# Heads: each step's products for the maxima stand behind the scores and the weighted sums

## The reference, cut to what matters

```python
def _L1_gnn_ref(x, adjacency, W_q, W_k, W_v, W_o, b_o):
    q = (x @ W_q).reshape(8, 2048, 4, 32).transpose(0, 2, 1, 3)
    k = (x @ W_k).reshape(8, 2048, 4, 32).transpose(0, 2, 1, 3)
    v = (x @ W_v).reshape(8, 2048, 4, 32).transpose(0, 2, 1, 3)
    scores = jnp.einsum('bhnd,bhmd->bhnm', q, k) / np.sqrt(32)
    scores = jnp.where(adjacency == 0, -jnp.inf, scores)
    attn = jax.nn.softmax(scores, axis=-1)
    out = jnp.einsum('bhnm,bhmd->bhnd', attn, v)
    return out.transpose(0, 2, 1, 3).reshape(8, 2048, 128) @ W_o + b_o

# layer 0: adjacency attention with scores that are sums of two node values
# layer 1:
h = jnp.maximum(_layernorm(x, axis=-1), 0.0)
x = x + _L1_gnn_ref(h, adj, ...)
# layers 2 and 3: mean over neighbours; adjacency attention again
```

## Time and profile before

| what | us |
|---|---|
| median of 3 runs (lowest, highest) | 3532.34 (3532.33, 3533.17) |
| the profiled execution | 3530.73 |
| its span, first to last instruction | 3528.9 |
| TensorE busy, products | 3409.4 (97%) |
| TensorE busy, weight loads | 1790.0 (51%) |
| VectorE busy | 3066.7 (87%) |
| GpSimd busy | 1830.4 (52%) |
| ScalarE busy | 1808.0 (51%) |
| the stage `heads`, first to last product | about 762 to 2643 |

### The profile page before, as it was taken

One profiled execution on the slowest core, in us unless ns is written; L12 is line 12 of the kernel. 1 busy time (PEld: TensorE's weight loads), 2 busy tenths in 40 slices (PEclk: granted clock), 3 DMA queues, 4 the chain that ended last, 5 costly groups with the idle time before them and its releaser, 6 DMA issues. The chain is left out here.

```text
span 3528.9 us, 58152 instructions
## 1 busy us (share of the span) xinstructions
PE 3409.4 (97%) x21140; PEld 1790.0 (51%) x21155; DVE 3066.7 (87%) x6862; ACT 1808.0 (51%) x4044; POOL 1830.4 (52%) x922
## 2 busy tenths in 40 slices
PE   6899998889999999999999999999998999899999
PEld 6799998431111111111111111111116999899999
DVE  8899997579999999999999999999977776677777
ACT  8633543766666666666666666666662554310010
POOL 7400101238888888888888888888870111000000
PEclk9999999999999999999999999999998999999999
DMA  8612121940011011101110111010003331312120
GB/s 301 220 69 91 55 91 54 291 161 10 25 30 30 8 27 30 30 6 29 30 30 5 30 30 30 6 30 30 6 7 108 120 120 73 121 67 91 55 91 25
DMA packets 78816, 234.62 MB, mean 66 GB/s; under 512 B 13504, under 2 KB 40768, under 8 KB 64448
## 3 DMA queue, kind: packets, MB, share of 16 engines
q1 hardware_dynamic: 77808, 230.56, 19.5%
q10 hardware_dynamic: 720, 0.33, 0.0%
HBM read 148.85 MB, written 81.99 MB: 65 GB/s over the span
## 5 line engine op out<-in xcount | busy, mean ns | idle before, releaser
L1828 POOL TENSOR_TENSOR a_w<-a_w,keep_mask_t 128x1024 f32<-128x1024 f32 x760 | 1608.0, 2141 | 306.1 <-ACT a_w L1813 306.1
L1813 ACT ACTIVATE a_w<-a_sc_ps 128x512 f32<-128x512 f32 x2048 | 1111.4, 595 | 705.1 <-PE a_sc_ps L1734 703.5
L1712 PE MATMUL a_o_ps<-a_w,a_v 128*33 128x512 f32 x4096 | 1079.1, 605 | 0.2
L1191 PE MATMUL g_acc<-g_hv,g_w 128*128 128x129 f32 x8192 | 923.2, 276 | 16.6 <-DVE g_w L1036 16.6
L1191 PEld LDWEIGHTS g_acc<-g_hv,g_w 128*128 128x128 f32 x8192 | 920.8, 193 | 17.9 <-ACT g_hv L1069 13.3
L1767 DVE CUSTOM_DVE_ANT_0 a_mx_ps<-a_mx_ps,a_mbias 128x512 f32<-128x512 f32 x1024 | 673.9, 718 | 39.5 <-PE a_mx_ps L1696 39.0
L1767 DVE CUSTOM_DVE_ANT_0 a_mx_ps<-a_mx_ps,em_mbias 128x512 f32<-128x512 f32 x968 | 636.5, 718 | 30.1 <-PE a_mx_ps L1696 29.8
L1734 PE MATMUL a_sc_ps<-a_qs,a_ks 97*128 97x512 f16 x2048 | 621.8, 385 | 0.5 <-ACT a_w L1813 0.2
L1780 DVE TENSOR_TENSOR a_w<-a_w,keep_mask_t 128x1024 f32<-128x1024 f32 x264 | 468.6, 1775 | 22.0 <-ACT a_w L1813 16.6
L1696 PEld LDWEIGHTS a_mx_ps<-a_ks,a_qs 32*128 32x128 f16 x1992 | 88.8, 91 | 784.9 <-DVE a_mx L1767 428.0
L1036 DVE SCALAR_TENSOR_TENSOR g_w<-f_row,keep_s,keep_mask_t 128x1024 f32<-128x1024 f32 x256 | 331.9, 1318 | 71.7 <-PE g_acc L1191 67.7
(11 more groups left out here) (313 smaller groups left out, 2383.2 us busy)
## 6 DMA issues: line engine op xcount, KB each, us to landing
p_adj_in<-in_adj SPq DMA_DIRECT2D x16, 1024.0 KB, 8.8
v<-p_v SPq DMA_DIRECT2D x32, 264.0 KB, 3.2
a_v<-v SPq DMA_DIRECT2D x16, 528.0 KB, 3.6
f_row<-u_rows SPq DMA_DIRECT2D x16, 512.0 KB, 5.9
g_x<-in_x SPq DMA_DIRECT2D x8, 1024.0 KB, 11.2
g_row<-u_rows SPq DMA_DIRECT2D x16, 512.0 KB, 8.1
x<-ho_o SPq DMA_DIRECT2D x16, 512.0 KB, 3.0
a_ks<-k_hi SPq DMA_DIRECT2D x64, 128.0 KB, 2.9
```

Of the source, the lines that this page charges most:

```text
L1191: mm = nc.tensor.matmul(tile(half, it), w[:, g % PB, it * P:(it + 1) * P], hv[:, k, jt, :], start=(jt == 0 and it % 3 == 0), stop=(jt == T ...
L1712: mm = nc.tensor.matmul(o_ps[2 * HD * a:2 * HD * a + HD + 1, c % 2, :], v[u][:, jt, a, :], w[:, g % PB, a, :], start=(jt == 0), stop=(jt = ...
L1813: nc.scalar.activation(w[:, g % PB, a], sc_ps[:, n % SB], ACT.Exp, scale=SCALE).then_inc(exp_done, 1)
L1828: nc.gpsimd.tensor_tensor(w[:, g % PB], w[:, g % PB], keep["mask_t"][:, jt, c * BANK:(c + 1) * BANK].unsqueeze(1).to_broadcast([P, 2, BANK ...
```

## The change

In the step loop of TensorE the first slot of a step was issued in front of its scores, and any further slot behind its weighing. Now all slots of a step are issued behind its weighing. The wait for the queries and keys of the next pair (`qk_loaded`) stays in front of everything, the wait for the placed shifts (`shift_placed`) stays in front of the scores. The code of the other engines is the same. The numbers of lines behind L1727 go down by one: the scores are L1733, the maximum on VectorE L1766, its mask L1779, the exponentials L1812, GpSimd's mask L1827.

```diff
@@ -1724,7 +1724,6 @@
                     if jt == 0 and tc == 0 and chunk < CHUNKS * B:
                         pe.wait_ge(qk_loaded[tu], LOADS * (i + on + 1))
                     mine_now = of_step(jt)
-                    slot(mine_now[0], chunk, tu, tc)
                     if jt == 0:
                         pe.wait_ge(shift_placed, 32 * (CHUNKS * i + g // T + 1))
                     for a in range(2):
@@ -1738,7 +1737,7 @@
                         weigh(g - LAG, i)
                     elif i > 0:
                         weigh(BODY + g - LAG, i - 1)
-                    for k in mine_now[1:]:
+                    for k in mine_now:
                         slot(k, chunk, tu, tc)
```

## The result

| | before | after |
|---|---|---|
| median of 5 runs, us | 3532.34 (3529.83 to 3533.57) | 3549.01 (3547.35 to 3551.49) |
| profiled execution, its span | 3530.73, 3528.9 | 3548.99, 3547.1 |
| the stage, start of its first to start of its last product | 1881.5 | 1897.1 |

The ratio is 1.0047, with an interval of 1.0036 to 1.0058: slower by 17 us. Of the 18.3 us between the profiled executions 15.6 lie in the stage, 0.6 ahead of it and 2.0 behind it.

The account below looks back on a forecast made before the run. TensorE's own stream was taken to bound the kernel. Only the steps around the turn cost, 63 x 0.21 = +13.3 us on 3530.73, giving 3544.0; 1.6 to the median made it 3545.6, say 3546, range 3537 to 3584.

Parts of the forecast that it names:

- (a): Ordinary steps on TensorE: the three gaps between products stay, so 14 of 16 steps cost what they did; cost 0.
- (b): Steps around the turn of the row maxima, on TensorE: 0.21 us more per chunk, 63 times, +13.3 us.
- T to M4: Gap from the turn of row maxima to step 4's maxima products: 0.20 or 0.21 us claimed, 63 times.
- (c, d): VectorE's mask asks at +1.49 us after step 2's scores, 0.16 before GpSimd, and takes 1.22; cost 0.
- rival 3: GpSimd takes the shared ports first, VectorE waits a whole instruction and TensorE waits: +330 us, 3862 us; chance 0.08.
- (e): Step 4's maxima products need step 3's maximum on VectorE taken first, for its buffer: slack 0.11 us, cost 0.
- rival 2: Step 3's maxima on VectorE are late at the turn: 63 x 0.2 to 0.7 more, 3558 to 3590; chance 0.14.
- (f): Shifts' DMA, placed some 1.4 us later, stays covered; the stage's start and end cost below 0.5 us.
- The sum: Whole kernel: profiled 3530.73 + 13.3 = 3544.0 us; as that execution lies 1.6 below the median, 3545.6, say 3546.
- Rival 1: The weight load of step 4's maxima products hides under the turn, gap 0.11: +7 us, 3539; chance 0.13.
- Rival 4: Faster: part of the 0.99 from weighing to maxima products waits for VectorE; -28, some 3518 us; chance 0.05.
- W to M: Gap on TensorE from the weighing to the maxima products, 0.98 or 0.99 us; claimed to hold no wait for VectorE.

Follow-up runs that it names:

- E2: Changed kernel with the small turn of the row maxima put between its step's scores and weighing; 3546.32 us, ratio 1.0038.
- E7: Kernel with maxima products in pairs and the turn between scores and weighing, GpSimd masking only one of two heads; 3491.07 us, ratio 0.9882.
- E6: Changed kernel, VectorE's masks also waiting for the second exponential of the next step, asking 0.03 ahead of GpSimd; 3555.37 us, ratio 1.0060.
- E5: Changed kernel, VectorE's masks also waiting for the first exponential two steps later, when GpSimd holds the ports; 3915.26 us, ratio 1.1082.
- E4: Changed kernel with a 128x256 memset on VectorE ahead of each of its masks; 3557.81 us, ratio 1.0071.
- E3: Kernel before, with GpSimd multiplying the mask onto only one of two heads; 3531.66 us, ratio 0.9996.
- E1: Changed kernel with the turn back in front of its step's scores, all maxima products alone behind the weighing; 3563.84 us, ratio 1.0091.
- P1: Changed kernel with maxima products in pairs (even step's behind weighing, next odd step's before scores) and the turn before its scores; 3510.03 us, ratio 0.9939.

## Why the prediction was right, point by point

- *The ordinary step costs nothing* (a): right. 14 of 16 steps kept 0.320, 0.535 and 0.986 within 0.001 us.
- *The turn's step costs 0.21* (b): right in place and size. T to M4 is 0.205, the total 0.209. It was counted 63 times, with the last turn, which has no M4 behind it; 62 are right. That it is a switch of 0.10 on top of T's 0.11 was taken from one nearest row; E2 and E7 show it by moving the same turn to a place without one, where it costs 0.111. The Trainium skill's rule (TensorE: Matmul & The Clock Gate, section Step-by-step: what each phase is for), read as covering M4's load under T, would have given 0.11 from T to M4; the 55 undisturbed places with 0.205 are against that reading. So is the load's own record, which stands beside M4 in all 62 places.
- *VectorE first at the ports* (c, d): right. The mask asks at +1.48 (predicted +1.49; in the other half of the chunks the lead is larger still), GpSimd at +1.65, the masks take 1.22, GpSimd's first of three 3.04. Against rival 3 the lead was ample: E6 shows that 0.04 is enough. Its price was of the right size but for the clock (E5).
- *Slack of M4 0.11* (e): it is 0.03 in one half of the chunks, those from which it was worked out, and 0.14 in the other (E4, E6). The sum left out the 0.057 from the maximum's end to the start of M4. So the slack held by less than I had worked out, and "cost 0" failed in 7 of 62 places. At the start of graphs 2 to 8 VectorE idles 0.23 ahead of its maximum of step 3 and M4 loses 0.31: 2.2 us that the sum lacked. This is a small piece of rival 2. Why VectorE is late there the profile doesn't show, and I did not test it.
- *The shifts' DMA and the stage's ends* (f): right. The gaps show no wait for the shifts, and start and end of the stage lose 0.4 together (below 0.5 predicted).
- *The sum*: 13.3 predicted, 16.7 by the medians and 18.3 by the profiled executions. The 18.3 as measured: turns 13.0, late maxima 2.2, the stage's ends 0.4, ahead of the stage 0.6, the stretch with the clock spell in the third layer 2.0, 0.1 unassigned. Of the 5 us above the predicted 13.3, half (0.6 and 2.0) has nothing to do with the change's mechanism.
- *Rival 1*: out (0.205, not 0.11). *Rival 4*: out, by E3 and by W to M, which kept its 0.986 with VectorE 61 us idler.
- One thing that I overlooked did no harm here: T, too, waits for a buffer. Behind W it has room, behind M3 or in front of a pair it has none (E1, P1).

## What to carry to other kernels

In a stream that bounds the kernel, count the changes between kinds of product, not only the products: here a reordering that leaves each engine's work the same paid 0.10 us wherever it split a pair or put unlike products side by side, and pairing them on purpose gained 22 us. When one is won, look at what stands a tenth of a microsecond behind it, here a buffer and then the ports that VectorE and GpSimd share. A wait that a trace names on a weight load need not be a loss (428 us of them moved no product here); the gap between products with and without it decides.

## What the runs showed of the hardware

- The change between kinds of product costs 0.09 to 0.10 us: between 32-row pairs and products over 97 or 128 rows (T to M 0.205, T to S 0.109), and also between these and the weighing with 33 columns (S to W 0.535, but S to T 0.442). None inside a kind: M to M 0.226, S to T, T to S. Where it is paid, the weight load is recorded beside its product, where it is not, well ahead of it (T to M 0.004 us in all 62 places after, T to S 0.107 in all 63 before).
- VectorE and GpSimd exclude each other for whole instructions in these multiplications (1.22 against 1.90 or 2.06 us for the mask, E3 and E5), and a recorded lead of 0.04 us suffices (E6). With a memset just ahead of the mask VectorE went first even at a recorded lag of 0.04 to 0.15 us, in 226 of 264 masks (E4); so the recorded starts alone don't decide, and what does stays open.
- A product for the maxima starts 0.057 us behind the end of VectorE's read that frees its buffer, where it waits for it (E4, E6).
- TensorE's clock fell to its lower level, 1.2 GHz, 24 times in E5's stage, where the engine was busy 783 of 900 us (mean 0.98). In every other version it was at 1.00 behind the stage's first 11 us.
